# Pair attention on one core: where TensorE's queue has the score products of the preceding step, behind both halves of the first layer or between them

## The reference

```python
p = x[:, ROW, :]
q = x[:, COL, :]
inner = p * q
h = jax.nn.relu(jnp.einsum('bpe,he->bph', inner, W1) + b1)
logits = jnp.einsum('bph,oh->bpo', h, W2) + b2
attn = jax.nn.softmax(logits, axis=1)
pooled = jnp.sum(inner * attn, axis=1)
return pooled @ Wl.T + bl
```

## Time and profile before

| what | value |
|---|---|
| median of 3 runs | 1135.3 us (1134.89 to 1136.12) |
| the profiled execution, its own time | 1135.53 us |
| its span in the trace | 1133.7 us |
| mean granted TensorE clock | 0.996 of full speed |
| TensorE matmul busy | 1121.1 us, 99% of the span |
| VectorE busy | 1042.1 us, 92% |
| ScalarE busy | 982.5 us, 87% |

### The profile page before, as it was taken

The page is one execution under the profiler, slowest core; times in us unless marked ns, Lnnn a source line. Parts: engine busy times, 40 slices in busy tenths (PEclk is TensorE's granted clock), DMA queues, the critical chain, the costliest instruction groups (busy, mean ns, idle before and its releaser), DMA issues.

```text
span 1133.7 us, 63855 instructions
## 1 busy us (share of the span) xinstructions
PE 1121.1 (99%) x29021; PEld 560.9 (49%) x29021; DVE 1042.1 (92%) x1679; ACT 982.5 (87%) x1220; POOL 0.7 (0%) x6
## 2 busy tenths in 40 slices
PE   9999999999999999999999999999999999999996
PEld 5444544445545444454455444444554545544442
DVE  8999989899898998989999898998989989899892
ACT  6889888888888889888888888888889888898885
POOL 0000000000000000000000000000000000000000
PEclk9999999999999999999999999999999999999998
DMA  3121221222212221212212213131131221212110
GB/s 76 25 68 29 63 41 26 67 41 54 39 30 63 41 56 37 52 43 40 64 29 43 56 34 70 25 68 35 29 69 30 62 41 25 68 36 58 29 18 31
DMA packets 220379, 51.35 MB, mean 45 GB/s; under 512 B 216016, under 2 KB 216016, under 8 KB 220112
## 3 DMA queue, kind: packets, MB, share of 16 engines
q1 hardware_dynamic: 219456, 47.11, 20.3%
q10 hardware_dynamic: 656, 0.16, 0.1%
HBM read 34.11 MB, written 13.12 MB: 42 GB/s over the span
## 4 chain that ended last, share of the span: by engine, by line
PE 92%; DVE 7%; issue 0%; ACT 0%; POOLq 0%; POOL 0%; DVEq 0%; ACTq 0%
PE slot L299 56%; PE logit_bank L319 28%; DVE inner L465 6%; PE slot L281 4%; PE slot L268 4%; DVE inner L473 0%; PE logit_bank L328 0%; DVE x_scaled L448 0%; ACT hidden L387 0%; DVE weighted L516 0%; DVE xt L439 0%; DVE row_max L502 0%; DVE logits L483 0%; PE slot L352 0%; DVE stats L505 0%
## 5 line engine op out<-in xcount | busy, mean ns | idle before, releaser
L387 ACT ACTIVATE hidden<-slot,b_col 128x780 f32<-128x780 f32 x1024 | 875.9, 910 | 120.1 <-PE slot L299 120.1
L465 DVE TENSOR_TENSOR inner<-xt 128x760 f32<-128x760 f32 x1024 | 911.2, 946 | 1.1
L299 PE MATMUL slot<-inner,w_block 64*32 64x390 f32 x16384 | 787.8, 488 | 0.2 <-DVE inner L465 0.2
L299 PEld LDWEIGHTS slot<-inner,w_block 64*32 64x32 f32 x16384 | 319.8, 107 | 330.3 <-issue 254.3
L319 PE MATMUL logit_bank<-hidden,w_window 64*32 64x390 f32 x8192 | 449.3, 487 | 1.2 <-DVE logits L483 0.7
L319 PEld LDWEIGHTS logit_bank<-hidden,w_window 64*32 64x32 f32 x8192 | 159.3, 105 | 178.4 <-ACT hidden L387 80.5
L483 DVE COPY logits<-logit_bank 128x780 f32<-128x780 f32 x15 | 14.6, 971 | 60.9 <-PE logit_bank L319 60.9
L473 DVE TENSOR_TENSOR inner<-xt 128x80 f32<-128x80 f32 x256 | 60.4, 236 | 0.0
L370 ACT COPY xt<-slot 128x640 f32<-128x640 f32 (+1 forms) x65 | 44.5, 686 | 13.8 <-PE slot L268 13.8
L268 PEld LDWEIGHTS slot<-ident,x_rows 128*128 128x128 f32 x320 | 34.1, 141 | 40.2 <-issue 39.4
L281 PE MATMUL slot<-xt,x_scaled 64*40 64x40 f32 x4096 | 52.9, 205 | 0.6 <-DVE x_scaled L448 0.6
(11 more groups left out here) (38 smaller groups left out, 33.5 us busy)
## 6 DMA issues: line engine op xcount, KB each, us to landing
x_rows<-in_r_x SPq DMA_DIRECT2D x127, 160.0 KB, 3.0
gram<-gram_dram SPq DMA_DIRECT2D x32, 400.0 KB, 3.7
gram_dram<-gram_rows SPq DMA_DIRECT2D x512, 12.5 KB
gram_dram<-gram_rows SPq DMA_DIRECT2D x256, 25.0 KB
x_rows<-in_r_x ACTq DMA_DIRECT2D x1, 160.0 KB, 3.3
w_rows<-in_L_rec_W SPq DMA_DIRECT2D x2, 16.0 KB, 2.6
wl_col<-in_L_rec_Wl SPq DMA_DIRECT2D x2, 0.2 KB, 2.4
b_col<-in_L_rec_b SPq DMA_DIRECT2D x2, 0.2 KB, 2.3
```

The source lines that it names most:

```text
L299: last = nc.tensor.matmul(banks[to:to + QUAD, ab * BANK:ab * BANK + HALF], w1_block[rows, of:of + QUAD], inner[rows, at:at + HALF], start= ...
L387: nc.scalar.activation(hidden[s % RING][:, half * PAIRS:(half + 1) * PAIRS].rearrange("p (a n) -> p a n", a=2), banks_of("layer", s, half) ...
L465: nc.vector.tensor_tensor(window_view(inner, to + half * HALF, [[PAIRS, STEP_DUOS], [SPAN, SHIFTS], [1, SPAN]]), window_view(fields, at + ...
```

## The change

TensorE issues the scores of the preceding step between the two halves of the first layer. Nothing else is changed: no instruction is added or taken out, and the queues of the other engines are the same.

```diff
             for s in range(STEPS):
                 first_layer(s, 0)
-                first_layer(s, 1)
                 if s:
                     score(s - 1)
+                first_layer(s, 1)
                 if s in turn_after:
                     turn_chunk(turn_after[s])
                 if s in gram_after:
```

## The result

The changed kernel takes 1420.6 us (median of 4 runs, 1419.6 to 1421.6) against 1135.4 us before: a ratio of 1.251, with a 95% interval from 1.2495 to 1.2525. It is slower by 285 us. The growth was forecast as 314 us and is 285. The miss lies in one term of the plain step, the time from a half's first matmul to its relu, which recurs 446 times.

A forecast was written before the change was run, and what follows sets the result against it. TensorE, with matmuls busy 99% of the span, was taken as the bound. To 1133.7 us, 446 plain steps x 0.71 added 316.7; smaller terms made 1447.1 of span, 1449 us in all, range 1427 to 1485.

The forecast's parts named there:

- The path of a plain step: From L1(s) through relu(s,1) and S(s) to L1(s+1), L0(s+1) beside the relu: 2.68 us, up 0.71 from 1.97.
- L1 starts to relu starts: 1.05 us: In a plain step, time from a second half's first matmul to its relu: 1.05 us.
- relu start to scores: In a plain step, relu of 0.91 us plus 0.06 us from its end to the scores' first matmul.
- scores to L1: In a plain step, time from the scores to the next group behind them: 0.66 us.
- wake-up of TensorE: Relu's end to the scores' first matmul: 0.06 us, read from one row; hardly under 0, perhaps 0.25 us.
- Chunk steps at no cost: In chunk steps transposes and Gram products cover the relu: no stop before the scores, added cost 0.
- Is ScalarE really free?: Check that relus, exponentials and Gram copies on ScalarE delay no relu in the new order: cost 0.
- The stops for VectorE: TensorE's stops for VectorE vanish: 0.56 us at first scaled rows, 0.68 at step 33, 2.0 in later rounds.
- The ends: Start and end of the kernel: +0.12 us at the start, -0.15 us at the last relu.
- The clock rival: Stops in each step bring TensorE to 1.2 GHz: about 2360 us, or some 1900 at half the time; chance 0.03.
- TensorE stepping over the waiting scores: Rival: TensorE runs the ready L1(s+1) while S(s) waits, so not slower: 1132 to 1135 us; chance 0.02.
- What would show it: Signs in the new profile: plain steps 2.68 us, stops some 210 us, TensorE near 84% busy, chunk steps 3.6 us.

The follow-up runs named there:

- experiment 4: Changed kernel with relu(s, 1) run twice, once into a tile nobody reads: 1814.5 us.
- experiment 5: Changed kernel with relu(s, 1) from step 4 on over half of its numbers (128x390), result not the reference's: 1276.9 us.
- experiment 6: Changed kernel with the scores of the step before the preceding one between the halves: 1134.8 us.
- Experiments 1: Changed kernel with relu(s, 1) given the same second wait, for old scores, that relu(s, 0) has: 1451.1 us.
- experiment 2: Changed kernel with both waits on both relus, the filled slot first, then the old scores: 1420.4 us.
- experiment 3: Kernel before the change with relu(s, 0) no longer waiting for the old scores: 1135.3 us in a single execution.
- experiment 10: Kernel before the change with the new order only in the 64 steps that follow a chunk step: 1142.3 us.
- experiment 7: Changed kernel with the scores of the preceding step ahead of both halves: 1806.0 us.
- Experiment 12: Kernel before the change, scores of each round's first step (but the first round's) issued one step later: 1134.5 us.

## Why the prediction was wrong, point by point

**The path of a plain step: right.** S waits for relu(s, 1), L0(s+1) lies beside it, nothing else is done meanwhile; shown by the rows after and by experiments 4, 5 and 6.

**"L1 starts to relu starts: 1.05 us": the step that failed.** It is 0.97. The 1.05 was read before relu(s, 0), where the relu has two waits, the late one behind the other; relu(s, 1) has one. Experiments 1 to 3 show 0.06 us for that, and the rest is the difference between 1.03 and 1.05 that rows of the same kernel have among themselves. The other terms were off by 0.01 and 0.02 in opposite directions: relu start to scores 0.96 for 0.97, scores to L1 0.68 for 0.66. Together 2.61 for 2.68; 446 x 0.07 = 31 us, which takes 1449 to 1418. The prediction said that 0.01 us in the step is worth 4.5 us, and yet its range let the whole step be no more than 0.05 us shorter. The row that would have told was in the trace of the kernel before: there relu(2, 0) and relu(3, 0), which have no second wait either, start 0.99 and 0.97 us after their half (12.91 to 13.90 and 14.90 to 15.87 us). The second of them:

```profile
14.90 1.52 PE L299 MATMUL slot<-inner,w_block 64*32 64x390 f32 x32
...
15.87 1.71 ACT L387 ACTIVATE hidden<-slot,b_col 128x780 f32<-128x780 f32 x2 [0.25 <-PE slot L299]
```

The prediction does name 2.61 us and 1418 us once, as its lower end with a wake-up of TensorE of nothing. That this is the measured step is chance: by its own terms that end is 2.68 - 0.06 = 2.62 us and 1422 us, and the wake-up is still there, 0.05 us.

**The remaining 2.6 us** are mostly in five plain steps, whose scores are 2.92 to 3.22 us from the next instead of 2.61, 2.2 us in all (at 13, 151, 261, 546 and 656 us). In them L1 and L0 are drawn apart, and the trace names no engine as the cause. This stays open.

**Chunk steps at no cost: right**, 3.59 us and no wait.

**"Is ScalarE really free?": right for this kernel**: the wait before the scores is 0.41 or 0.42 us in steps with an exponential too. But experiment 10 shows how thin the margins are, and experiment 7 that the handover of 0.81 us between relus binds as soon as both relus lie on the path.

**The stops for VectorE: gone, as said.** In the waits of the changed kernel, TensorE no longer waits for the copy of the logits or for the scaled rows, and the steps at the round starts, which took 2.08 us and more before, take 2.61 like the others. Experiment 12 got back only 1 us from the same stops, since its own order lost some. VectorE itself waits more (74% busy), at no cost that the trace shows.

**The ends: right in kind, wrong in size.** The last relu starts 0.97 us after L1(511), 1407.32 against 1406.35:

```profile
1406.35 0.86 PE L299 MATMUL slot<-inner,w_block 64*32 64x390 f32 x16
...
1407.32 0.91 ACT L387 ACTIVATE hidden<-slot,b_col 128x780 f32<-128x780 f32 x1 [0.90 <-PE slot L299]
...
1408.28 0.89 PE L319 MATMUL logit_bank<-hidden,w_window 64*32 64x390 f32 x16 [1.07 <-ACT hidden L387]
```

From L1(511) to the last scores it was 2.38 us before (1120.28 to 1122.66) and is 1.93 now, 0.45 less where the prediction had 0.15. Its "1.20" for the old start of that relu was 1.42: relu(511, 0), which went ahead of it, began 1.28 us after its half, not 1.05. That is 0.3 us of the sum.

**The clock rival: refuted here.** The granted clock is 1.00 from 100 to 1400 us of the changed kernel, and in experiments 4 and 7 with stops three times as long. The rule of the Trainium skill that was weighed, TensorE: Matmul & The Clock Gate, in "A second HAM failure mode: psum-queue depth-cycling", does not show itself here: stops of 0.41 us in each 2.61, and of 1.27 in each 3.47, leave the clock at 2.4 GHz. That section of the Trainium skill tells of another kernel, with bf16 data and 512 columns.

**TensorE stepping over the waiting scores: refuted.** L1, which was ready, starts behind them: in the rows above it comes 0.68 us after S, and the plain steps take 2.61 us.

**What would show it:** TensorE's stops 184.8 us (said: some 210) and 86% busy (said: 84%), the chain through L387 (29%), chunk steps of 3.6. The 2.68 was not found, and the smaller stops and the higher busy share follow from it; it was the number on which the range stood.

## What to carry to other kernels

When a queue is bound by one engine, count for each wait how much of that engine's other work lies between the request and the wait, and compare it with the whole round trip: here 0.66 us against 1.93. Take each term of such a round trip from the very instruction that will be exposed, with the same number and order of waits, since a term that recurs 446 times turns 0.07 us into 31. And where ScalarE waits for two semaphores in front of an ACTIVATE, as here, write the one that is satisfied last first.

## What was not expected of the hardware

- On ScalarE, a second semaphore wait costs 0.06 us per instruction if the late one stands second in the program, and nothing if it stands first: 1451.1 against 1420.4 us with the same waits.
- Half a group of products (four of eight, 64x32 tiles with 390 columns) takes TensorE as long as the whole group: 0.65 us, with 8 matmul instructions as with 16. Leaving out half of the scores in 480 steps gained nothing (1137.4 against 1135.4 us).
- TensorE can stand empty for 1.2 to 1.3 us of every 3.4 to 3.5 over a whole run without a lower granted clock.
